# Local attention in a fused recurrent/attention kernel: a ring of key blocks, and the query norm as the scale of the exponentials

## The reference

```python
q = l2norm(q) * qs
k = l2norm(k) * ksc
q, k = rotary_xpos(q, k)              # cos, sin and a scale per position
bq = q.reshape(b, h, w, WINDOW, d) * QK_SCALE      # WINDOW = 64, QK_SCALE = 8
bk, bv = (look_around(bk), look_around(bv))        # the block before, and its own
sim = jnp.einsum('bhwid,bhwjd->bhwij', bq, bk)
sim = jnp.where(mask, -jnp.finfo(sim.dtype).max, sim)
attn = jax.nn.softmax(sim, axis=-1)
out = jnp.einsum('bhwij,bhwjd->bhwid', attn, bv)
```

## Time and profile before

| | |
|---|---|
| median of 3 runs | 1334.16 us (1333.44 to 1335.03) |
| the profiled execution's own time | 1331.52 us |
| its span in the profile | 1329.7 us, 38195 instructions |
| TensorE busy | 1261.0 us, 95% |
| TensorE weight loads | 1009.5 us, 76% |
| VectorE busy | 1107.6 us, 83% |
| ScalarE busy | 1160.4 us, 87% |
| GpSimd busy | 1133.9 us, 85% |
| DMA | 70.05 MB, mean 53 GB/s |

### The profile page before, as it was taken

The page is one execution under the profiler, slowest core; times in us unless marked ns, Lnnn a source line. Parts: engine busy times, 40 slices in busy tenths (PEclk is TensorE's granted clock), DMA queues, the critical chain, the costliest instruction groups (busy, mean ns, idle before and its releaser), DMA issues.

```text
span 1329.7 us, 38195 instructions
## 1 busy us (share of the span) xinstructions
PE 1261.0 (95%) x13793; PEld 1009.5 (76%) x13794; DVE 1107.6 (83%) x1924; ACT 1160.4 (87%) x3529; POOL 1133.9 (85%) x831
## 2 busy tenths in 40 slices
PE   7889999999999998999988999999999999999997
PEld 4777888888888887666756788888888888876775
DVE  6788888888888886688878999998899999984777
ACT  5878999999999998776768899999999999998886
POOL 4888999999999987376689999999999999984775
PEclk9999999999999999999999999999999999999999
DMA  5222222222322211010011111111222111110222
GB/s 165 53 54 61 69 61 61 61 73 65 80 70 54 53 38 34 16 44 25 1 29 38 45 45 45 46 45 46 51 51 50 46 46 45 37 38 25 77 76 86
DMA packets 60299, 70.05 MB, mean 53 GB/s; under 512 B 8912, under 2 KB 38288, under 8 KB 60112
## 3 DMA queue, kind: packets, MB, share of 16 engines
q1 hardware_dynamic: 60112, 67.61, 20.2%
HBM read 13.33 MB, written 4.19 MB: 13 GB/s over the span
## 4 chain that ended last, share of the span: by engine, by line
PE 73%; ACT 7%; issue 5%; POOL 5%; DVE 5%; DMA 2%; SPq 1%; ACTq 0%; DVEq 0%; POOLq 0%
PE ps L182 58%; PE ps L243 8%; PE ps L253 3%; PE ps L256 3%; ACT P L631 3%; POOL t L1219 2%; DMA norm<-X 1%; POOL hxr L1219 1%; DVE t L947 1%; POOL P L1219 1%; DVE t L956 1%; DVE nm L975 1%; ACT sqk L605 1%; DVE sums L963 1%; ACT Vn L645 1%
## 5 line engine op out<-in xcount | busy, mean ns | idle before, releaser
L631 ACT ACTIVATE P<-ps,nm 128x128 f32<-128x128 f32 x1024 | 363.5, 384 | 3.9 <-DVE nm L975 3.9
L182 PE MATMUL ps<-wqkv,hT 128*128 128x512 f32 x1152 | 326.9, 426 | 13.1 <-DVE t L947 10.0
L1219 POOL TENSOR_TENSOR P<-P,rden 128x512 f32<-128x512 f32 x256 | 296.2, 1164 | 43.7 <-DVE rden L982 42.9
L1219 POOL TENSOR_TENSOR t<-t 128x1024 f32<-128x1024 f32 x128 | 307.1, 2399 | 30.2 <-DVE t L947 28.9
L182 PEld LDWEIGHTS ps<-wqkv,hT 128*128 128x128 f32 x1152 | 214.8, 188 | 89.6 <-issue 28.1
L1219 POOL TENSOR_TENSOR t<-t,rr 128x1024 f32<-128x1024 f32 x128 | 243.4, 1901 | 16.5 <-ACT rr L614 16.4
L631 ACT ACTIVATION_READ_ACCUMULATOR P<-ps,nm 128x1 f32 x1024 | 230.9, 226 | 0.0
L1219 POOL TENSOR_TENSOR hxr<-hxf,hxr 128x512 fp32r<-128x512 f32 (+1 forms) x94 | 128.6, 1396 | 87.3 <-ACT hxr L687 87.3
L956 DVE TENSOR_TENSOR t<-ps,tabl 128x512 f32<-128x512 f32 x256 | 164.2, 683 | 38.5 <-ACT sqk L605 38.1
L621 ACT ACTIVATE PT<-ps 128x1024 f32<-128x1024 f32 x128 | 130.4, 1019 | 63.3 <-PE ps L243 62.2
L975 DVE TENSOR_REDUCE nm<-ps 128x4 f32<-128x512 f32 x256 | 173.7, 680 | 5.1 <-PE ps L182 5.1
(11 more groups left out here) (131 smaller groups left out, 2553.6 us busy)
## 6 DMA issues: line engine op xcount, KB each, us to landing
Vs<-Vn SPq DMA_DIRECT2D x224, 128.0 KB, 2.3
side<-in_x SPq DMA_DIRECT2D x16, 256.0 KB, 3.0
A<-X SPq DMA_DIRECT2D x16, 256.0 KB, 2.5
norm<-X SPq DMA_DIRECT2D x32, 128.0 KB, 2.3
oT<-in_x SPq DMA_DIRECT2D x16, 256.0 KB, 2.9
out<-oT SPq DMA_DIRECT2D x16, 256.0 KB, 2.2
norm<-X SPq DMA_DIRECT2D x32, 127.8 KB, 2.4
hsh<-X SPq DMA_DIRECT2D x31, 128.0 KB, 2.2
```

The lines of the kernel that those rows point to most:

```text
L182: return e.matmul(o, lhsT, rhs, start=start, stop=stop, skip_group_check=True)
L631: k = act(P[:, g, :], ps[:, 3 + s, (g % 4) * 128:(g % 4 + 1) * 128], ACT.Exp, bias=nm[:, g:g + 1], accum_out=den[:, g:g + 1])
L1219: return e.tensor_tensor(o, a, b_, op)
```

## The change

The keys lie in a ring of five blocks of 64 per head pair: tile t writes blocks (2t+1) mod 5 and the next one; a window reads two neighbouring blocks, or, where it wraps, blocks 0 and 4 as one two-piece operand, with mask and V in the matching order. The copy between slots is gone. The queries are no longer scaled by their inverse root: GpSimd scales only the keys. The inverse root of the query norm is instead the scale operand of the eight exponentials, and VectorE multiplies the negated row maximum by it, after a semaphore wait for its own reduction. rr has two copies, since the exponentials of a tile come after the next tile's root; norm_rt waits accordingly. The q transposes wait only for the add.

```diff
@@ sbuf
-        rr = sb("rr", [128, 16])
+        rr = sb("rr", [128, 2, 16])
+        mx8 = sb("mx8", [128, 8])
-            kT = sp_("kT", [128, 4, 64 + 256])
+            kT = sp_("kT", [128, 4, 5, 64])
+        def q_root(n):
+            return rr[:, n % 2, 0:8].rearrange("p (c s) -> p s c", s=2)
+        def windows(t, w):
+            k = (2 * t + w) % 5
+            return slice(k, k + 2) if k < 4 else slice(0, 5, 4)
@@ TensorE, turn_qk
-                e.wait_ge(s_tn, n + 1)
+                e.wait_ge(s_add, n + 1)
...
                 k.then_inc(s_tpq, 1)
+                e.wait_ge(s_tn, n + 1)
@@ TensorE, sims
-                            k0 = (t % 2) * 128 + w * 64
-                            k = mm(ps[64 * w:64 * w + 64, 3 + hh, c * 128:(c + 1) * 128], qT[p, c, 64 * w:64 * w + 64],
-                                   kT[p, c, k0:k0 + 128], False, True)
+                            k = mm(ps[64 * w:64 * w + 64, 3 + hh, c * 128:(c + 1) * 128].rearrange("p (s k) -> p s k", s=2),
+                                   qT[p, c, 64 * w:64 * w + 64], kT[p, c, windows(t, w), :], False, True)
@@ ScalarE, norm_rt
-                if n:
-                    e.wait_ge(s_tn, n)
-                act(rr[:], ss[:], ACT.Ln, scale=65536.0).then_inc(s_rr0, 1)
+                if n > 1:
+                    e.wait_ge(s_tn, n - 1)
+                    e.wait_ge(s_e, 2 * n - 2)
+                act(rr[:, n % 2, :], ss[:], ACT.Ln, scale=65536.0).then_inc(s_rr0, 1)
@@ ScalarE, exps
+                e.wait_ge(s_rr, n + 1)
                 e.wait_ge(s_nm, 2 * n + s + 1)
                 for g in range(4 * s, 4 * s + 4):
                     k = act(P[:, g, :], ps[:, 3 + s, (g % 4) * 128:(g % 4 + 1) * 128], ACT.Exp,
-                            bias=nm[:, g:g + 1], accum_out=den[:, g:g + 1])
+                            scale=q_root(n)[:, s, g % 4:g % 4 + 1], bias=nm[:, g:g + 1], accum_out=den[:, g:g + 1])
@@ VectorE, row_max
-                e.tensor_reduce(nm[:, 4 * s:4 * s + 4], S4, AX, ALU.max, negate=True).then_inc(s_nm, 1)
+                e.tensor_reduce(mx8[:, 4 * s:4 * s + 4], S4, AX, ALU.max, negate=True).then_inc(s_mx, 1)
+                e.wait_ge(s_rr, n + 1)
+                e.wait_ge(s_mx, 2 * n + s + 1)
+                e.tensor_tensor(nm[:, 4 * s:4 * s + 4], mx8[:, 4 * s:4 * s + 4], q_root(n)[:, s, :], ALU.mult).then_inc(s_nm, 1)
@@ VectorE, keep_k
-                if t == 2:
-                    e.wait_ge(s_kt, n)
-                    e.tensor_copy(kT[:, :, 0:64], kT[:, :, 256:320])
-                e.tensor_copy(kT[:, :, s0:s0 + 128], ps[:, 6, :].rearrange("p (c q) -> p c q", c=4)).then_inc(s_kt, 1)
+                e.tensor_copy(kT[:, :, k0:k0 + 2, :], ps[:, 6, :].rearrange("p (c w q) -> p c w q", c=4, w=2)).then_inc(s_kt, 1)
@@ GpSimd, scale_qk
-                v = heads(tq[i % 2])
+                v = heads(tq[i % 2])[:, HEADS:, :]
...
-                tt(v, v, rr[:].unsqueeze(2).to_broadcast([128, 16, DH]), ALU.mult).then_inc(s_tn, 1)
+                tt(v, v, rr[:, n % 2, HEADS:].unsqueeze(2).to_broadcast([128, HEADS, DH]), ALU.mult).then_inc(s_tn, 1)
@@ SP, shift_v
+                old, new = HALF[::-1] if 2 * t % 5 == 4 else HALF
                 if t:
-                    e.dma_start(Vs[0:64, t, :], Vn[64:128, t - 1, :]).then_inc(s_vlo[t], 16)
-                e.dma_start(Vs[64:128, t, :], Vn[0:64, t, :]).then_inc(s_vhi[t], 16)
+                    e.dma_start(Vs[old[0], t, :], Vn[64:128, t - 1, :]).then_inc(s_vlo[t], 16)
+                e.dma_start(Vs[new[0], t, :], Vn[0:64, t, :]).then_inc(s_vhi[t], 16)
```

More of the change, by code:

```diff
@@ L52, in program @@
         idb = sb("idb", [128, 128], BF16)
-        mask = sb("mask", [128, 2, 128], BF16)
+        mask = sb("mask", [128, 4, 64], BF16)
         cst = sb("cst", [128, 8])
@@ L143, in end_bank, with masks @@
             return 7 if b < NB - 3 else 3 + b - (NB - 3)
+        def windows(t, w):
+            k = (2 * t + w) % 5
+            return slice(k, k + 2) if k < 4 else slice(0, 5, 4)
+        def masks(t, w):
+            if t == 0 and w == 0:
+                return slice(0, 2)
+            return slice(2, 4) if (2 * t + w) % 5 < 4 else slice(1, 3)
         HALF = (slice(0, 64), 0), (slice(64, 128), 1)
@@ L167, in program @@
             sem(n_) for n_ in ("s_dec", "s_rt0", "s_rt", "s_osq", "s_rms0", "s_rms", "s_s", "s_th"))
-        s_cst, s_tabm, s_t2, s_ss0, s_ss, s_nm, s_rd, s_kt, s_wlo, s_w2lo, s_h0, s_hxlo1 = (
-            sem(n_) for n_ in ("s_cst", "s_tabm", "s_t2", "s_ss0", "s_ss", "s_nm", "s_rd", "s_kt", "s_wlo", "s_w2lo", "s_h0", "s_hxlo1"))
+        s_cst, s_tabm, s_t2, s_ss0, s_ss, s_mx, s_nm, s_rd, s_kt, s_wlo, s_w2lo, s_h0, s_hxlo1 = (
+            sem(n_) for n_ in ("s_cst", "s_tabm", "s_t2", "s_ss0", "s_ss", "s_mx", "s_nm", "s_rd", "s_kt", "s_wlo", "s_w2lo", "s_h0", "s_hxlo1"))
         s_bn, s_st, s_dcy, s_dk, s_xadd, s_hc, s_hn, s_b1g, s_gh, s_oa = (
@@ L269, in sims @@
                         mm(ps[64 * w:64 * w + 64, 3 + hh, :].rearrange("p (c k) -> p c k", c=4), idb[p, p],
-                           mask[p, min(t + w, 1), :].unsqueeze(1).to_broadcast([64, 4, 128]), True, False)
+                           mask[p, masks(t, w), :].rearrange("p s k -> p (s k)").unsqueeze(1).to_broadcast([64, 4, 128]), True, False)
                 for c in range(4):
@@ L609, in norm_rt @@
                 e.wait_ge(s_ss, n + 1)
-                if n:
-                    e.wait_ge(s_tn, n)
-                act(rr[:], ss[:], ACT.Ln, scale=65536.0).then_inc(s_rr0, 1)
+                if n > 1:
+                    e.wait_ge(s_tn, n - 1)
+                    e.wait_ge(s_e, 2 * n - 2)
+                act(rr[:, n % 2, :], ss[:], ACT.Ln, scale=65536.0).then_inc(s_rr0, 1)
                 e.wait_ge(s_rr0, n + 1)
-                act(rr[:], rr[:], ACT.Exp, scale=-0.5, bias=ln2x8).then_inc(s_rr, 1)
+                act(rr[:, n % 2, :], rr[:, n % 2, :], ACT.Exp, scale=-0.5, bias=ln2x8).then_inc(s_rr, 1)
             def keep_p(l, i):
@@ L985, in keep_k @@
                 n, t = l * NT + i, i % TPB
-                s0 = 64 + (t % 2) * 128
+                k0 = (2 * t + 1) % 5
                 e.wait_ge(s_tpk, n + 1)
@@ L1293, in no_tile @@
                     e.memset(P[:, 0:2, :], 0.0)
-                e.memset(kT[:, :, 0:64], 0.0)
+                e.memset(kT[:, :, 0, :], 0.0)
                 e.memset(Vs[0:64, 0, :], 0.0).then_inc(s_zero, 1)
@@ L1503, in constants @@
     k = np.arange(128)[None, :]
-    ok = (k >= q) & (k <= q + 64)
-    first = ok & (k >= 64)
-    mask = np.where(np.stack([first, ok], 1), f(0.0), f(-1e30))
+    ok = ((k >= q) & (k <= q + 64)).reshape(64, 2, 64)
+    first = ok & (np.arange(2)[None, :, None] == 1)
+    mask = np.where(np.concatenate([first, ok], 1), f(0.0), f(-1e30))
     mask = np.concatenate([mask, mask], 0).astype(f)
```

## The result

The changed kernel takes 1534.6 us (median of 4 runs, 1533.1 to 1537.8) against 1334.6 for the kernel before; the ratio is 1.150, with a 95% interval of 1.148 to 1.152. It is 200 us slower. The forecast was 1550.

What follows compares the result with a forecast made beforehand. TensorE was taken to set the pace before the change. Layer 0 +114, layer 1 +106 and starts -3 gave +217 on 1331.5 us, 1548.5; forecast median 1550, own range 1485 to 1612, low end extended to 1460.

Steps and rivals of the forecast that it cites:

- The held product: VectorE's two-SBUF-input product stands until GpSimd's instruction is over; each tile's second waits 1.8 us for the add.
- exposes the add: GpSimd's halved scaling is over at about T+2.9 (T: q copy's end), so the second product meets the 2.39 us add.
- The ring of 9.12 us: Waits closing through VectorE, GpSimd and ScalarE: a tile takes at least 9.12 us instead of 7.77 or 8.07.
- Delays on top: First products behind other GpSimd work, port conflicts: 1.7 us a block in layer 0, 2.4 in layer 1.
- the starts: At the two starts of the attention loops GpSimd's halved scaling is on the chain: 3 us off.
- What closes the ring: On ScalarE, the second four exponentials wait for the second product, with the q copy and squares behind them.
- The scale operand: Per-partition operand on 1024 ScalarE exponentials: 0.092 us each, 0.37 for four, 2.95 a block.
- the product slips past: Rival, chance 0.07: the four-column product isn't held, ScalarE is the bound, 1378 us.
- Ring and half scaling: Slot copies go, worth 0.80 us a block in layer 1, 12.8 in all; two-piece windows and halved scaling cost nothing.
- TensorE stays the bound: Rival, chance 0.05: the 0.80 us wait ahead of layer 1's scores goes, plus 3 at the starts: 1318 us.
- The late add: Rival, chance 0.06: GpSimd's adds start after the second product, leaving a short wait: 1420 to 1480 us.
- The signs named: VectorE above 90%, TensorE near 80%, exponentials' idle for the product about 1 us a tile, blocks 38 us.

Runs made afterwards that it cites:

- The extra operation in the old kernel: Kernel before, plus an unused VectorE product (128x4, two SBUF inputs) after each row maximum: 1530.3 us; its control with one SBUF input: 1338.2 us.
- the swap for one input: Changed kernel, product replaced by a 128x4 reduction with one SBUF input, scale operand a column of ones: 1375.8 us, ratio 1.031.
- the two half kernels: Changed kernel, scale operand a column of ones, only one of the two products with two SBUF inputs: first alone 1397.8 us, second alone 1505.0 us.
- the missing scale operand: Changed kernel with no scale operand on the exponentials, product of two SBUF inputs kept (second a column of ones): 1520.0 us, ratio 1.139.
- the ring alone: Changed kernel with the root part put back: q and k both scaled on GpSimd, no scale operand, no product: 1331.4 us, ratio 0.997.
- the one with neither cost: Changed kernel, product replaced by a reduction of one SBUF input and no scale operand on the exponentials: 1327.7 us, ratio 0.993.

## Why the prediction was right

*The held product.* It was forecast to stand until GpSimd is through, 1.8 us in the second half of a tile. It takes 1.79 us and ends 0.02 after the add. The extra operation in the old kernel, the swap for one input and the two half kernels show it as the cause: 129 us of it in the second half, 22 in the first, 159 together. What the prediction had in excess here is the part of the halved scaling, which "exposes the add": the old kernel with the extra operation has the full scaling and loses 194 us. Since the trace of before had two such rows, this was the weakest support of the sum.

*The ring of 9.12 us.* Measured, 9.21 in a plain tile. It is a floor, as forecast: in the middle of the loops, no tile of either layer takes less than 9.19 from one q copy to the next. Of its terms, the first product starts 0.10 to 0.11 us after the reduction's end instead of 0.04 (the second one starts as late, but it waits for the add anyway), the exponentials start 0.12 after the second product instead of 0.07, and the q copy is 0.05 shorter; all others are within 0.02. I took the first price from a similar step, whose wait for its own reduction stands first of two and whose reduction reads SBUF; here the wait stands second and the reduction reads PSUM, and which of them makes the difference was not tried.

*Delays on top.* I estimated 1.7 and 2.4 us a block, for 38.2 and 38.9; blocks are 38.4 and 38.2. The first is right for partly another reason than named, which is luck: besides the first product's wait behind other GpSimd work (1.04 us at 332.61), TensorE waits for VectorE's addition of the projection. In layer 1, 0.7 us a block, 11 us in all, is too much. For the starts I gave 3 back; about 8 came, in the first and last blocks of the loops, and whether the halved scaling has a part in that was not tried. Against that layer 0 was 3 us too low. The sum of +217 met +204, and the forecast of 1550 was 15 us high. In the side sum for the scale operand, the ends (0.078 and 0.106) lie 0.014 and not 0.007 from 0.092; the 7 us are right all the same, since only four of a tile's eight exponentials lie in the ring.

*What closes the ring.* "On ScalarE, the second four exponentials wait for it, with the q copy and the squares behind them" holds for plain tiles, as 8.84 against 9.21 shows. That all tiles run this way was wrong. In layer 1 VectorE's own load is the bound (from 900 to 1270 us its waits for others come to 3.8 us); the prediction worked it out as 37.1 us a block (measured, 382.88/400 of 38.2, or 36.6) and then used it only to support a middle value. So the 2.4 us of delay on the ring is a right size for a wrong mechanism in layer 1, and that it came within 0.7 is partly luck. This didn't move the sum, but it made me expect 47 us from the missing scale operand, and 15 came.

*The scale operand.* 0.092 us each was forecast: in the median the exponentials stand 0.435 apart for 0.342, and the operand costs 48 us where no product is held. The rival "the product slips past" was priced at 1378, and the kernel that makes it true takes 1375.8.

*Ring and half scaling.* As costed: the stall of 0.80 us goes where TensorE is the bound, and the two-piece windows cost nothing in the median. The median of the ring alone gave 3.4 us of the 12.8; why its runs scatter over 9 us stays open. The rival "TensorE stays the bound" at 1318 has its closest kernel in the one with neither cost, 1327.7.

*The late add* did not come about: 121 of 128 second products wait for nearly the whole add. The first product, forecast free but for delays, is held in 48 tiles.

*The signs named.* VectorE "above 90%" holds inside layer 1 (96%) and just about in layer 0 (90%), not over the span (87%). TensorE is at 85% and not near 80, and ScalarE's wait for the product is 0.8 us a tile (106.6/128) and not 1.

## What to carry to other kernels

Before a small operation is put on VectorE, ask how many of its inputs lie in SBUF and what GpSimd does at that moment. With two SBUF inputs, four columns cost as much as the rest of the GpSimd instruction under way, and everything queued behind them pays too; with one input they cost 0.16 us, and the cosine product, which reads PSUM and one table in SBUF, keeps its 1.22 us beside GpSimd's scaling. The saving on GpSimd's side is not what exposed the product: with the full scaling kept, the extra operations were held for longer in all. Look at how much of a tile GpSimd is busy, and where in that the small operation falls.

A per-partition scale on many small ACTIVATEs is not free: 0.09 us each is a quarter of the distance between exponentials of 128 columns. The change should be split: the ring is worth keeping (3.4 us in the median), the root in this form is not.

## What the runs showed of the hardware that was not expected

The wait for a result of the same engine has more than one price: the next instruction starts 0.04 us after the end in the sums of the norm, and 0.10 after it behind the row maximum (median of 256 each), alike for the product and for the one-input reduction in its place. The one-input operation added to the kernel before does not wait for the row maximum ahead of it, and it starts 0.08 us before that one's end.

After a held product the engine goes on at once, but GpSimd's next instruction can pay in turn: where VectorE's two-input L1035 comes first, two normalisations take 2.48 us in place of 2.06, in the timeline of GpSimd of the changed kernel:

```profile
300.41 2.06 POOL L1237 TENSOR_TENSOR P<-P,rden 128x512 f32<-128x512 f32 x2 [1.54 <-DVE rden L1003]
...
318.85 2.48 POOL L1237 TENSOR_TENSOR P<-P,rden 128x512 f32<-128x512 f32 x2 [1.54 <-DVE rden L1003]
```

L1035 runs from 319.71 to 320.44 there, from the end of the first into the second. The second one alone takes 1.47 us in place of 1.04, in 14 blocks of layer 0. No normalisation of that trace is lengthened beside a product of four columns alone.
